# A selective scan on one core: units of two states instead of one, with decays and u products in SBUF

## What is computed

```python
dt = softplus(dt @ dt_w.T + dt_b)                   # step sizes, [image, t, 64]
dA = exp(dt[..., None] * A)                         # decays, A is one constant per state
dBx = dt[..., None] * Bm[:, :, None, :] * xc[..., None]   # the "u product": B times (dt * xc)
def step(h, inp):
    dA_t, dBx_t, C_t = inp
    h = dA_t * h + dBx_t                            # the scan, over t = 0..575, h starts at 0
    y = einsum('bds,bs->bd', h, C_t)                # weighing by C and the sum over 16 states
    return (h, y)
y = (ys + xc * D) * silu(z)                         # the gate
```

## Time and profile before

| | |
|---|---|
| median of 3 runs | 899.14 us (898.27 to 904.83) |
| profiled execution, its own time | 901.04 us |
| its span, first to last instruction | 899.3 us |
| busy: DVE, PE, POOL, ACT | 721.3, 708.9, 516.2, 369.3 us |
| scan loop, first L527 to the end of the last L941 | 302.1 to 805.5 us |

### The profile page before, as it was taken

The page is one execution under the profiler, slowest core; times in us unless marked ns, Lnnn a source line. Parts: engine busy times, 40 slices in busy tenths (PEclk is TensorE's granted clock), DMA queues, the critical chain, the costliest instruction groups (busy, mean ns, idle before and its releaser), DMA issues. The chain is left out here.

```text
span 899.3 us, 19137 instructions
## 1 busy us (share of the span) xinstructions
PE 708.9 (79%) x7722; PEld 442.3 (49%) x7722; DVE 721.3 (80%) x938; ACT 369.3 (41%) x585; POOL 516.2 (57%) x407
## 2 busy tenths in 40 slices
PE   7987886699877387788878878887887787787696
PEld 3554553356554154544544544454454454446363
DVE  3998887763320489999999989999999999974998
ACT  2220002156536755545555555555455554321000
POOL 5000000000010489999999999999999999970043
PEclk9999998889989799999999999999999999998799
DMA  4000000000004256666666665666667666600001
GB/s 162 5 4 4 5 4 2 3 1 1 1 1 126 74 171 210 197 187 190 212 194 188 197 203 177 189 209 196 189 189 213 187 198 205 195 30 1 0 12 41
DMA packets 55866, 102.81 MB, mean 114 GB/s; under 512 B 11169, under 2 KB 13345, under 8 KB 55777
## 3 DMA queue, kind: packets, MB, share of 16 engines
q1 hardware_dynamic: 55552, 100.73, 36.6%
q0 software_dynamic: 224, 0.85, 0.2%
HBM read 98.00 MB, written 3.54 MB: 113 GB/s over the span
## 5 line engine op out<-in xcount | busy, mean ns | idle before, releaser
L546 POOL TENSOR_TENSOR ring<-ring,big 128x576 f32<-128x576 f32 x206 | 285.1, 1406 | 13.7 <-DVE ring L936 11.8
L184 PE MATMUL banks<-ring,main_params 128*128 128x288 f32 x824 | 244.2, 426 | 4.6 <-POOL ring L546 2.8
L936 DVE TENSOR_TENSOR_SCAN ring<-big,banks 128x576 f32<-128x576 f32 x154 | 202.6, 1340 | 2.3
L184 PEld LDWEIGHTS banks<-ring,main_params 128*128 128x128 f32 x824 | 146.4, 192 | 60.0 <-POOL ring L546 15.7
L924 DVE TENSOR_TENSOR banks<-banks,big 128x576 f32<-128x576 f32 x192 | 143.0, 745 | 24.0 <-PE banks L1218 21.4
L718 ACT ACTIVATE big<-big,small 128x576 f32<-128x576 f32 x192 | 142.2, 764 | 27.3 <-DVE ring L936 21.5
L523 POOL COPY big<-normed 128x288 f32<-128x288 f32 x8 | 3.0, 429 | 244.2 <-DVE normed L422 244.2
L1217 PE MATMUL banks<-big,selectors 96*128 96x512 bf16 x192 | 74.5, 390 | 80.0 <-DVE ring L936 37.4
L356 PE MATMUL banks<-big 32*32 32x288 f32 x3712 | 96.9, 429 | 21.3 <-issue 17.2
L790 DVE SCALAR_TENSOR_TENSOR big<-big 128x288 f32<-128x288 f32 x216 | 93.6, 512 | 0.0
L718 ACT ACTIVATE banks<-big,small 128x576 f32<-128x576 f32 x64 | 47.4, 741 | 108.2 <-DVE ring L936 86.9
(11 more groups left out here) (166 smaller groups left out, 962.5 us busy)
## 6 DMA issues: line engine op xcount, KB each, us to landing
big<-bc_rows SPq DMA_DIRECT2D x640, 144.0 KB, 3.2
bc_rows<-big SPq DMA_DIRECT2D x16, 144.0 KB, 2.4
residual<-x_in SPq DMA_DIRECT2D x2, 576.0 KB, 5.8
out<-big SPq DMA_DIRECT2D x2, 512.0 KB, 3.0
main_params<-main_in SPq DMA_DIRECT2D x1, 895.0 KB, 8.7
big<-front_in POOLq DMA_DIRECT2D x1, 574.5 KB, 5.7
experts<-experts_in SPq DMA_DIRECT2D x1, 512.0 KB, 9.0
row_selectors<-rows_in POOLq DMA_DIRECT2D x1, 256.0 KB, 5.9
```

The source lines that it names most:

```text
L184: last = nc.tensor.matmul(PS[rows, 2 * p + a, 0:HALF], lhsT, rhs[:, bass.ds(at + a * HALF, HALF)], start=start, stop=stop, skip_group_chec ...
L546: nc.gpsimd.tensor_tensor(slot, slot, CT[n % 10], ALU.mult).then_inc(weighted, 1)
L936: nc.vector.tensor_tensor_scan(slot, DECAY[m % 3], place, 0.0, ALU.mult, ALU.add).then_inc(scanned, 1)
```

## The change

The loop runs over NPAIRS = 128 units k of two neighbouring states, 1152 columns, eight units per image (HS = 8):

- One DVE scan per unit over both states: DECAY[k % 3], three buffers of 1152 columns, and the slot, in place. The first column of each state's decay is set to 0 once before the loop (a memset on POOL), so the second state starts anew; ACT writes columns 1 to 575 of each state only, still one activation per state. All decays are in SBUF.
- One u product per unit. DVE's six of an image read B from PSUM banks 0 to 3 and write to the slot in SBUF; POOL's two (units 3 and 7) read BT and write to the slot. DTX is read twice through a zero stride.
- One weighing per unit on POOL, 1152 columns.
- PSUM homes are fixed: banks 0 to 3 for the B rows of one unit (free again when its u product is done), banks 4 and 5 for v_rows and bc_rows, banks 6 and 7 for y. The list USERS, place_of and wait_place are gone.
- Seven slots of two states (four in the ring, MORE, and two in XN, which is free by then), four C buffers and two B buffers of two states. A DMA spreads two rows at once; there are half as many. STAGE has two buffers instead of three.
- The places of step_sizes, the softplus steps, v_rows, bc_rows and the copies in the order of each engine are written out anew for units.

```diff
...
-        CT = [big(L) for _ in range(10)]
-        BT = [big(L) for _ in range(3)]
-        DECAY = [big(L) for _ in range(3)]
+        CT = [big(2 * L) for _ in range(4)]
+        BT = [big(2 * L) for _ in range(2)]
+        DECAYS = big(6 * L)
+        DECAY = [DECAYS[:, 2 * i * L:2 * (i + 1) * L] for i in range(3)]
...
         TMP = [big(L) for _ in range(2)]
-        MORE = [big(L) for _ in range(2)]
+        MORE = big(2 * L)
...
-        SLOT = [RING[:, i * L:(i + 1) * L] for i in range(8)] + MORE
+        SLOT = ([RING[:, 2 * i * L:2 * (i + 1) * L] for i in range(4)] + [MORE] +
+                [XN[:, 2 * i * L:2 * (i + 1) * L] for i in range(2)])
...
-        POOL_U = (3, 7, 11, 15)
-        V_AFTER, BC_AFTER = 1, 9
-        AHEAD = 2
+        SPARE_PAIR = 2
+        POOL_U = (3, 7)
+        POOL_AHEAD = (3, 2)
+        SIZES_AT = 3
...
-        def row(p):
-
-            return PS[:, 2 * p:2 * p + 2, :].rearrange("p a c -> p (a c)")[:, 0:L]
+        def rows_pair():
+
+            return PS[:, 0:4, :].rearrange("p (y a) c -> p y (a c)", y=2)[:, :, 0:L]
...
+        def twice(t):
+
+            return t.unsqueeze(1).to_broadcast([128, 2, L])
+
+        def wait_slot(engine, k):
+
+            if k >= SLOTS:
+                engine.wait_ge(y_added, 2 * (k - SLOTS + 1))
...
+                    rows = BCD[b, w, d, s:s + count].rearrange("s t -> (s t)")
+                    sp.dma_start(dst[d * DI:(d + 1) * DI, :], rows.unsqueeze(0).to_broadcast([DI, count * L])).then_inc(loaded, 16)
+
+            def load_b(k):
+                m = POOL_PAIRS.index(k)
+                if m >= 2:
+                    sp.wait_ge(u_pool, m - 1)
+                spread_rows(BT[m % 2], k // HS, 0, 2 * (k % HS), 2, b_loaded[m % 2])
+
+            def load_c(k):
+                if k >= 4:
+                    sp.wait_ge(weighted, k - 3)
+                spread_rows(CT[k % 4], k // HS, 1, 2 * (k % HS), 2, c_loaded[k % 4])
...
+            nc.gpsimd.memset(DECAYS.rearrange("p (y t) -> p y t", t=L)[:, :, 0:1], 0.0).then_inc(firsts_zero, 1)
...
-            def inputs_on_pool(n):
...
-                nc.gpsimd.tensor_tensor(SLOT[n % SLOTS], BT[m % 3], DTX[n // DS % 2], ALU.mult).then_inc(u_pool, 1)
-
-            def weigh(n):
-                pool.wait_ge(scanned, n + 1)
-                pool.wait_ge(c_loaded[n % 10], 32 * (n // 10 + 1))
-                slot = SLOT[n % SLOTS]
-                nc.gpsimd.tensor_tensor(slot, slot, CT[n % 10], ALU.mult).then_inc(weighted, 1)
...
+                nc.gpsimd.tensor_tensor(both(SLOT[k % SLOTS]), both(BT[m % 2]), twice(DTX[k // HS % 2]), ALU.mult).then_inc(u_pool, 1)
...
+                pool.wait_ge(scanned, k + 1)
+                pool.wait_ge(c_loaded[k % 4], 32 * (k // 4 + 1))
+                nc.gpsimd.tensor_tensor(SLOT[k % SLOTS], SLOT[k % SLOTS], CT[k % 4], ALU.mult).then_inc(weighted, 1)
...
+            for k in range(NPAIRS + 1):
+                if k >= 1:
+                    weigh(k - 1)
+                for at, ahead in zip(POOL_U, POOL_AHEAD):
+                    if k < NPAIRS and k % HS == at - ahead:
+                        inputs_on_pool(k + ahead)
+                if k < NPAIRS and k % HS == SIZES_AT and k // HS + 1 < B:
+                    step_sizes(k // HS + 1)
...
-            def decay(n):
-                b, s = n // DS, n % DS
+            def decay(k, y):
...
-                if s in POOL_U:
-                    wait_place(act, ("tile", n))
-                    out = row(place_of(("tile", n)))
-                else:
-                    m = DVE_TILES.index(n)
-                    if m >= 3:
-                        act.wait_ge(scanned, DVE_TILES[m - 3] + 1)
-                    out = DECAY[m % 3]
-                nc.scalar.activation(out, DT[b % 3], ACT.Exp, scale=ANEG[:, s:s + 1]).then_inc(decay_set, 1)
+                if k >= 3:
+                    act.wait_ge(scanned, k - 2)
+                nc.scalar.activation(both(DECAY[k % 3])[:, y, 1:L], DT[b % 3][:, 1:L], ACT.Exp, scale=ANEG[:, s:s + 1]).then_inc(decay_set, 1)
...
+                if k + 2 < NPAIRS:
+                    for y in range(2):
+                        decay(k + 2, y)
+                if k < 0:
+                    continue
+                if b < B and j == 1:
+                    step_inputs(b, SPARE_PAIR)
+                if b < B and j == 3:
+                    stage_rows(b, SPARE_PAIR)
+                if b < B and j == 4:
+                    middle(b, SPARE_PAIR)
+                if b < B and j == 5:
+                    low(b, SPARE_PAIR)
+                if k // HS + 1 < B and j in (0, 2):
+                    for step in (j, j + 1):
+                        softplus(k // HS + 1, step)
...
-            def inputs_on_dve(n):
...
-                u = row(place_of(("tile", n)))
-                nc.vector.tensor_tensor(u, u, DTX[n // DS % 2], ALU.mult).then_inc(u_dve, 1)
-
-            def scan(n):
-                dve.wait_ge(decay_set, n + 1)
-                slot, place = SLOT[n % SLOTS], row(place_of(("tile", n)))
-                if n in POOL_TILES:
-                    dve.wait_ge(u_pool, POOL_TILES.index(n) + 1)
-                    nc.vector.tensor_tensor_scan(slot, place, slot, 0.0, ALU.mult, ALU.add).then_inc(scanned, 1)
+            def inputs_on_dve(k):
+                dve.wait_ge(b_spread, DVE_PAIRS.index(k) + 1)
+                dve.wait_ge(dtx_set, k // HS + 1)
+                wait_slot(dve, k)
+                nc.vector.tensor_tensor(both(SLOT[k % SLOTS]), rows_pair(), twice(DTX[k // HS % 2]), ALU.mult).then_inc(u_dve, 1)
+
+            def scan(k):
+                dve.wait_ge(decay_set, 2 * k + 2)
...
                 else:
-                    m = DVE_TILES.index(n)
-                    dve.wait_ge(u_dve, m + 1)
-                    wait_slot(dve, n)
-                    nc.vector.tensor_tensor_scan(slot, DECAY[m % 3], place, 0.0, ALU.mult, ALU.add).then_inc(scanned, 1)
+                    dve.wait_ge(u_dve, DVE_PAIRS.index(k) + 1)
+                slot = SLOT[k % SLOTS]
+                nc.vector.tensor_tensor_scan(slot, DECAY[k % 3], slot, 0.0, ALU.mult, ALU.add).then_inc(scanned, 1)
...
+            dve.wait_ge(firsts_zero, 1)
+            dve.wait_ge(z_mm, 2 * J)
+            for k in range(-1, NPAIRS):
+                if k >= HS and k % HS == 3:
+                    gate_image(k // HS - 1)
+                if k >= 0:
+                    scan(k)
+                if k + 1 in DVE_PAIRS:
+                    inputs_on_dve(k + 1)
...
-            def spread_b(n):
-                b, s = n // DS, n % DS
-                place = place_of(("tile", n))
-                wait_place(pe, ("tile", n))
-                if s == 0:
+            def spread_b(k):
+                b, i = k // HS, DVE_PAIRS.index(k)
+                if i >= 1:
+                    pe.wait_ge(u_dve, i)
+                if k % HS == 0:
...
-                lhsT = SEL[:, s * 128:(s + 1) * 128]
-                nc.tensor.matmul(PS[:, 2 * place, :], lhsT, SPLIT[b % 4][:, 0:BANK], start=True, stop=True)
-                nc.tensor.matmul(PS[:, 2 * place + 1, 0:L - BANK], lhsT, SPLIT[b % 4][:, BANK:L],
-                                 start=True, stop=True).then_inc(b_spread, 1)
...
+                for y in range(2):
+                    s = 2 * (k % HS) + y
+                    lhsT = SEL[:, s * 128:(s + 1) * 128]
+                    nc.tensor.matmul(PS[:, 2 * y, :], lhsT, SPLIT[b % 4][:, 0:BANK], start=True, stop=True)
+                    last = nc.tensor.matmul(PS[:, 2 * y + 1, 0:L - BANK], lhsT, SPLIT[b % 4][:, BANK:L], start=True, stop=True)
+                last.then_inc(b_spread, 1)
+
+            def add_states(k):
+                b = k // HS
+                if k % HS == 0:
...
                     pair_matmul(Y_PAIR, DDIAG, XC, b * L, stop=False)
-                pe.wait_ge(weighted, n + 1)
-                pair_matmul(Y_PAIR, par("ident"), SLOT[n % SLOTS], 0, start=False, stop=s == DS - 1).then_inc(y_added, 1)
...
+                pe.wait_ge(weighted, k + 1)
+                for y in range(2):
+                    pair_matmul(Y_PAIR, par("ident"), SLOT[k % SLOTS], y * L, start=False,
+                                stop=k % HS == HS - 1 and y == 1).then_inc(y_added, 1)
...
+            for k in range(-1, NPAIRS + 3):
+                j, b = k % HS, k // HS + PREPARED
+                if k + 1 in DVE_PAIRS:
+                    spread_b(k + 1)
+                if k >= 0 and b < B and j == 4:
+                    take_high(b, SPARE_PAIR)
+                if k >= 0 and b < B and j == 5:
+                    take_middle(b, SPARE_PAIR)
+                if k >= 3:
+                    add_states(k - 3)
+                if k >= 0 and b < B and j == 0:
+                    if b >= PREPARED + 1:
+                        pe.wait_ge(low_set, b)
+                    v_rows(b, SPARE_PAIR)
+                if k >= 0 and b < B and j == 2:
+                    pe.wait_ge(v_set, b + 1)
```

(45 more changed lines are left out.)

92 lines of the change are left out of this document (24 added, 68 removed).

## The result

| | before | changed |
|---|---|---|
| median of 4 runs | 898.7 us (896.8 to 904.8) | 1155.1 us (1152.0 to 1156.7) |
| ratio | | 1.283, interval 1.277 to 1.289 |
| span of the profiled execution | 899.3 us | 1154.8 us |
| per image (gates) | 31.02 us | 46.71 us |

The change makes the kernel 28% slower. The page, in the same columns as the earlier trace rows: POOL is now busy for 67% of the span, where it was 57%, and both long instructions last far longer on average than the 2.55 and 2.62 us that the prediction took for 1152 columns.

The account below looks back on a forecast made before the run. DVE and POOL, both nearly full side by side, bound the kernel. With exclusion, 787.9 us of turns plus a 3.4 us drain end the last gate 290.7 us later: 1190 us, by itself 1128 to 1230; overall range 915 to 1240.

Parts of the forecast that it names:

- What bounds the kernel: Scan loop before the change: POOL (29.9 us) and DVE (28.8 us) work side by side within 31.0 us per image.
- Both scan inputs in SBUF: All 128 scans beside POOL instructions reading SBUF: full exclusion, whole instructions taking turns, chance 0.70.
- The reduce: L443 on DVE, one SBUF input: takes 1.01 us beside POOL as well as with POOL idle, evidence for no delay.
- The sum: Scans, weighings, POOL's u products and step sizes in the loop add up; last gate 290.7 us later.
- Turns: In the loop, 128 scans x 2.55, 160 POOL instructions x 2.62 and 30 step-size instructions x 1.41: 787.9 us.
- the low end: Whole kernel at 1128 us: POOL's long instructions at 2.37 us (-40) and neighbouring turns overlapping slightly (-22).
- Drain: From the end of the loop's turns to the end of the last gate: 3.4 us.
- Before the loop, costed at nothing: Memset of first decay columns before the loop: no added time, as POOL is idle for 41.2 us before L527.
- Costed at nothing: Memset, new DVE and PE waits, ACT, PE and larger DMAs add no time; clock fall allowed 8 us, high only.
- No contention: Scan beside weighing in the loop: neither delays the other, POOL sets the pace, 867 to 885 us; chance 0.14.
- Sharing by the element: Scans and POOL instructions in the loop both continue, but slower, while overlapping: 1030 us, 910 to 1120; chance 0.11.
- A new wait: About 0.25 us per unit in the loop for late C or B rows, without contention: 899 us; chance 0.05.

Follow-up runs that it names:

- The runs with one edit each: Kernel before with POOL weighing two states per 1152-column instruction: ratio 1.001; kernel before with POOL's u products moved to states 0, 4, 8, 12: ratio 0.996.
- both together, with the u products in another order: Kernel before with 1152-column weighings, POOL states 0, 4, 8, 12, and their u products made between two weighings, three states ahead: 886.1 us, ratio 0.984.
- the four runs made from it: Changed kernel with scan decays from one PSUM column, 875.6 us; half the weighing, 1003.5; memset as weighing, 921.6; unit 7's u product three units ahead, 1150.2.

## Why the prediction was right, and where its sizes were off

**What bounds the kernel.** Right: two engines side by side, both nearly full. The runs with one edit each show it more sharply than the shares did: relieving either alone gives nothing clear of noise and 0.4%, both together, with the u products in another order, 1.6%. That order was not run without the other two edits.

**Both scan inputs in SBUF.** The step that decides, read from one 1.37 us row, held: exclusion, by whole instructions, cause and size shown from both sides (the run with PSUM decays takes it away, the run with u in the slot adds it alone). The reduce was no counterexample. But by the rows alone the step was a guess by likeness, and in so far it was luck: L918 reads one SBUF tensor, as L443 does, so "two streams instead of one" is not what tells these two rows apart. L918 showed that DVE and POOL can exclude each other; that a scan with two SBUF inputs does so was shown only by the result. No run has L918 without POOL beside it.

**The sum.** The predicted gate was 290.7 us later; the span grew by 255.5. The terms, from the profiled execution:

- Turns: 787.9 us predicted. They run from POOL's first u product, 310.27, to the last weighing's end, 1055.47: 745.2 us. This is the term that was mis-sized, by 42.7: it took whole durations where pitches add up. The durations were right (2.552 and 2.627 us, undisturbed), but a scan between two POOL instructions adds 2.28 us, not 2.55: 128 x 0.27 = 35. POOL's pitch is 2.57 instead of 2.62 and 1.36 instead of 1.41: 160 x 0.05 + 30 x 0.05 = 9.5. Together that is 44, where 42.7 was measured. I had put overlap at the turns into the low end only, with 22 us, when the pitches already showed that one duration is no pitch.
- Drain: 1059.31 - 1055.47 = 3.8 us, predicted 3.4.
- Before the loop, costed at nothing: the first L532 starts at 307.25 instead of 302.07, 5.2 us later. 0.7 of this is there at 272 us already; the rest is ACT waiting 5.25 us instead of 0.77 for one convolution product of PE. Before, then after, and PE's own idle time:

```profile
288.60 1.22 ACT L664 ACTIVATE big<-banks,main_params 128x1152 f32<-128x1152 f32 x1 [0.77 <-PE banks L1161]
...
293.78 1.22 ACT L670 ACTIVATE big<-banks,main_params 128x1152 f32<-128x1152 f32 x1 [5.25 <-PE banks L1160]
...
290.87 0.47 PE L1160 MATMUL banks<-normed,conv_weights 32*64 32x288 f32 x4 [3.17 <-issue]
```

  That code is the same in both kernels. PE stood for 3.17 us in which the profile shows nothing that it waited for. The pause is no accident of one execution: in front of L532 POOL is idle for 45.5 to 45.9 us in the changed kernel and the four runs made from it, against 41.2 in front of L527. Why PE paused is open; no run was made for it.
- After the last gate: 95.5 us instead of 93.8.

-42.7 + 0.4 + 5.2 + 1.7 = -35.4, where the difference is -35.2; the turns began another 0.1 us after step_sizes(0), and the rest is rounding.

**Costed at nothing.** No POOL wait for C rows shows in the loop; the larger DMA lands in 4.4 us, within the 7.7 us that it had. The clock fell, but only to 0.81 in the mean, and PE kept ahead: POOL and DVE wait for nothing of PE except the last gate.

**The rivals.** "No contention" was priced at 867 to 885 us; the run with PSUM decays came to 875.6. "Sharing by the element" is out: in the timeline one always ends before the other moves. "A new wait" took nothing.

## What to carry to other kernels

Before giving a VectorE instruction of two inputs both of them in SBUF, look at what GpSimd does in the same stretch: if it reads SBUF there, the two add up instead of overlapping, as scan, weighing and u product did here, and no wait in the profile says so, only durations that are too long. Price turns by pitch, not by duration. Where two engines are both nearly full, an edit that relieves one shows nothing; relieve both and check which queue each product stands in.

## What the hardware showed unexpectedly

- The turn is shorter than the instruction: a scan of 2.55 us adds 2.28 us to POOL's pitch, one of 576 columns (1.34 us) about 1.07 (a pitch of 2.43 between weighings, 1.36 without).
- Long POOL instructions save more than long DVE ones. Two POOL instructions of 576 columns have a pitch of 2.72, one of 1152 has 2.57; two DVE scans of 576 have 2.48, one of 1152 has 2.47 (600.98 to 603.45 in the run with PSUM decays). On POOL, reading one input twice through a zero stride costs next to nothing (2.633 against 2.627 us).
- An instruction that only writes, on POOL, is left alone by a scan with two SBUF inputs: 2.02 us, all 128 of them within 0.03, and the median scan takes 2.56.
